# Layer 0's experts of a two-layer AdaLN kernel: all eight by every token, or the two chosen ones by gathered rows

## Time and profile before

| | us |
|---|---|
| median of 3 runs | 474.52 (472.8 to 476.28) |
| the profiled execution | 476.3 |
| its span, first to last instruction | 474.5 |
| PE, DVE, ACT, POOL busy | 426.4, 360.9, 336.2, 252.9 |
| mean granted TensorE clock | 0.845 |

### The profile page before, as it was taken

How to read it: one execution, slowest core, us unless ns; L and a number is a source line. 1 busy time by engine, 2 the same in 40 slices (tenths; PEclk the granted TensorE clock), 3 DMA queues, 4 the chain that set the end, 5 groups by cost and what they waited for, 6 DMA issues and landing times.

```text
span 474.5 us, 7765 instructions
## 1 busy us (share of the span) xinstructions
PE 426.4 (90%) x2212; PEld 285.5 (60%) x2212; DVE 360.9 (76%) x891; ACT 336.2 (71%) x898; POOL 252.9 (53%) x276
## 2 busy tenths in 40 slices
PE   8979778899899899886999889969989999999995
PEld 6667666676567677652433335324447887787883
DVE  4766795867898879689858896995848777879763
ACT  3364558787688686778998889968946566585552
POOL 3302238786866776822443543443418964766663
PEclk9997998999999999995565555555569999999999
DMA  6730021121134643633058344203114342433640
GB/s 185 207 112 2 0 79 57 44 92 56 35 114 108 164 149 103 123 87 114 12 90 118 96 98 131 60 5 102 24 22 149 127 126 81 141 128 92 183 130 22
DMA packets 45675, 44.68 MB, mean 94 GB/s; under 512 B 5557, under 2 KB 33789, under 8 KB 45633
## 3 DMA queue, kind: packets, MB, share of 16 engines
q1 hardware_dynamic: 45632, 44.19, 34.5%
HBM read 37.73 MB, written 6.44 MB: 93 GB/s over the span
## 4 chain that ended last, share of the span: by engine, by line
PE 43%; DVE 13%; issue 5%; ACT 3%; POOL 1%; POOLq 0%; DVEq 0%; ACTq 0%
PE P L1244 8%; PE P L1245 8%; PE P L1246 8%; PE P L1523 8%; PE P L1513 5%; DVE nm L902 4%; PE P L1380 1%; ACT EX L1179 1%; POOL hidl L469 1%; PE P L1349 1%; PE P L1268 1%; DVE O L917 1%; PE P L1374 1%; DVE kvs L697 1%; DVE SC L606 1%
## 5 line engine op out<-in xcount | busy, mean ns | idle before, releaser
L469 POOL TENSOR_TENSOR hidl<-tmp,hidh 128x512 fp32r<-128x512 f32 x116 | 149.3, 1296 | 76.6 <-ACT hidh L1131 73.9
L1179 ACT ACTIVATE EX<-P,nm 128x256 f32<-128x256 f32 x256 | 116.9, 496 | 12.5 <-DVE nm L902 12.2
L1131 ACT ACTIVATE hidh<-tmp 128x512 fp32r<-128x512 f32 x116 | 73.1, 630 | 44.8 <-DVE tmp L865 20.4
L902 DVE TENSOR_REDUCE nm<-P 128x4 f32<-128x1024 f32 x64 | 77.8, 1218 | 24.4 <-PE P L1513 24.0
L1523 PE MATMUL P<-EX,qs 128*32 128x256 f32 x512 | 66.8, 619 | 12.1 <-DVE O L917 12.0
L1244 PE MATMUL P<-XH,WH 128*128 128x512 f32 x176 | 76.1, 433 | 1.5 <-DVE tmp L974 0.6
L1245 PE MATMUL P<-XH,WL 128*128 128x512 f32 x176 | 70.1, 399 | 0.0
L1246 PE MATMUL P<-XL,WH 128*128 128x512 f32 x176 | 70.1, 398 | 0.0
L513 POOL TENSOR_TENSOR qs<-qT,rz 128x128 f32<-128x128 f32 x64 | 24.6, 406 | 81.5 <-DVE rz L910 81.5
L865 DVE TENSOR_TENSOR tmp<-P,G 128x512 f32<-128x512 f32 x64 | 43.6, 687 | 25.2 <-ACT P L1152 20.1
L1244 PE MATMUL P<-hidh,WH 128*128 128x512 f32 x124 | 50.7, 409 | 11.3 <-POOL hidl L469 9.8
(11 more groups left out here) (138 smaller groups left out, 670.7 us busy)
## 6 DMA issues: line engine op xcount, KB each, us to landing
G<-gate_rows SPq DMA_DIRECT2D x56, 256.0 KB, 3.3
kv_parts<-kvs SPq DMA_DIRECT2D x16, 256.0 KB, 2.4
VS<-kv_parts SPq DMA_DIRECT2D x48, 64.0 KB
KS<-kv_parts SPq DMA_DIRECT2D x48, 64.0 KB
G<-gate_rows SPq DMA_DIRECT2D x8, 224.0 KB, 3.0
G<-gate_rows SPq DMA_DIRECT2D x8, 192.0 KB, 3.3
G<-gate_rows SPq DMA_DIRECT2D x8, 160.0 KB, 2.6
X<-in_x SPq DMA_DIRECT2D x4, 256.0 KB, 2.9
```

What stands on the lines that cost most here:

```text
L469: nc.gpsimd.tensor_tensor(hidl[:, u % 3, :], source, hidh[:, u % 3, :].bitcast(fp32), ALU.subtract).then_inc(s["low_ready"], 1)
L902: v.tensor_reduce(nm1[:, g % 4, 2 * h:2 * h + 2, :], P[:, bank:bank + 2, :].rearrange("p j (h s) -> p (j h) s", h=2), AX.X, ALU.max, negat ...
L1131: sc.activation(hidh[:, u % 3, :], source, ACT.Copy).then_inc(s["high_ready"], 1)
L1179: last = sc.activation(ex1(g, j)[:, h * S:(h + 1) * S], P[:, bank_s1(g, j), h * S:(h + 1) * S], ACT.Exp, bias=nm1[:, g % 4, j, h:h + 1], a ...
```

## The change

Layer 0's experts are computed for the chosen rows alone, in plain fp32:

- The shared expert stays dense: `shared_ups` and `shared_down` per pair, added to X by `shared_experts` on VectorE.
- Tokens are handled in two *waves* of 1024. For a wave, TensorE counts with a triangular matrix how many tokens ahead of each have chosen the same expert (`ranks`), and VectorE makes of it a slot number for each token and choice (`destinations`): each expert's rows start at a multiple of 128, so that 23 tiles of 128 rows hold any split of 2048 rows.
- GpSimd scatters the rows of a wave to DRAM with 16 indirect DMAs (`scatter`), SyncE loads them tile by tile, TensorE computes each tile with its expert's weights, whose column is read from a register (`wave_columns`), and SyncE stores the result in its place. GpSimd gathers the two rows of each token with indirect DMAs (`gather`); `combine` weights and adds them (VectorE for pairs 0 and 1, GpSimd for 2 and 3).
- The weights `W1`, `W2` are no longer split. The hidden bias is added by VectorE from `B1`, a broadcast of all biases. The DRAM areas are filled with zeros first.
- The norm, q, k and v of the second attention: pair 0 within wave 1 (steps 14 to 19), pairs 1 to 3 within the attention.

The core of the diff:

```diff
+WAVES = 2
+QPW = NP // WAVES
+TPW = NT // WAVES
+WTOK = TOK // WAVES
+TILES = 2 * WTOK // D + E - 1
+XGR = 4
...
+COMBINE_AT = 14
+KV_AT = 18
...  (SyncE)
+            load(tri[:, :], a["tri"], "ld_b")
+            load(tab[:, :], a["tab"].partition_broadcast(128), "ld_b")
...
+            for w in range(WAVES):
+                sp.dma_start(scratch["xe"][w].rearrange("(i p) d -> p i d", p=128),
+                             WT[:, 0, 0:D].unsqueeze(1).broadcast_to([128, TILES, D])).then_inc(filled, 16)
             sp.wait_ge(s["rows_ready"], 1)
...
             sp.wait_ge(s["rows_out"], 16)
-            for l, dst in ((0, mrow0), (1, mrow1)):
+            load(B1[:, :], a["ub0row"].partition_broadcast(128), "ld_w1")
+            for l, dst in ((0, mrow0), (2, mrow5), (1, mrow1)):
...
+            for n in range(XGR, WAVES * TILES + 7):
+                if n < WAVES * TILES:
+                    tile_load(n)
+                if n >= 7:
+                    tile_store(n - 7)
+                if n - 4 == TILES + KV_AT + 1:
+                    kv_store(0, 0)
+                if n - 4 == TILES + KV_AT + 2:
+                    kv_store(0, 1)
+                    kv_load(0)
+            kv_store(1)
+            kv_load(1)
...  (GpSimd)
+            def scatter(w):
+                pool.wait_ge(s["dest_ready"], w + 1)
+                pool.wait_ge(s["rows_sb"], QPW * (w + 1))
+                pool.wait_ge(filled, 16 * WAVES)
+                for t in range(TPW):
+                    for k in range(2):
+                        nc.gpsimd.indirect_dma_start(scratch["xe"][w], bass.IndirectOffsetOnAxis(dest[:, w, t, k:k + 1], 0),
+                                                     SC[:, TPW * w + t, :], None).then_inc(scattered[w], 16)
...
+            scatter(0)
+            root(1, 3)
+            scatter(1)
+            stored_tiles(0)
+            for p in range(QPW):
+                for t in range(TPP):
+                    for k in range(2):
+                        gather(p, t, k)
+                if p == 0:
+                    root(2, 0)
...
             for g in range(NG):
-                if g == 3:
-                    root(2, NP - 1)
+                if g == 1:
+                    root(2, 1)
+                if g == 0:
+                    stored_tiles(1)
+                if g < 6:
+                    p, n = 2 + g // 3, g % 3
+                    for j in range(3 * n, min(3 * n + 3, 2 * TPP)):
+                        gather(p, j // 2, j % 2)
+                if g in (4, 7):
+                    combine(2 + g // 7)
...  (VectorE, the destinations)
+                link(v.tensor_tensor(over[:, :, :], count.unsqueeze(2).broadcast_to([128, E, E]),
+                                     tab[:, 0:E].unsqueeze(1).broadcast_to([128, E, E]), ALU.is_gt))
...
+                v.tensor_copy(dest[:, w, :, :], slot[:, :, :]).then_inc(s["dest_ready"], 1)
...  (VectorE, the tiles)
+            for n in range(WAVES * TILES):
+                w, i = tile(n)
+                if n >= 3:
+                    tile_out(n - 3)
+                if n == TILES:
+                    at = wave_columns(1)
+                bias(n, at[i])
...
+                    if i == 11:
+                        destinations(1)
...
+                if w == 1:
+                    if i == COMBINE_AT:
+                        combine(0)
+                        ln_stats(2, 0)
...  (ScalarE, the tiles)
+            for n in range(WAVES * TILES):
+                w, i = tile(n)
+                if n + 1 < WAVES * TILES:
+                    tile_in(n + 1)
+                if n >= 1:
+                    tile_back(n - 1)
+                tile_hidden(n)
...  (TensorE, the tiles)
+            tile_transpose(0)
+            for n in range(WAVES * TILES):
+                w, i = tile(n)
+                if n + 1 < WAVES * TILES:
+                    tile_transpose(n + 1)
+                if n == TILES:
+                    at[1] = wave_columns(1)
+                tile_up(n, at[w][i])
+                if n >= 1:
+                    tile_turn(n - 1)
+                if n >= 2:
+                    tile_down(n - 2, at[(n - 2) // TILES][(n - 2) % TILES])
+                if w == 0:
+                    if i == 1:
+                        route(0, 3)
+                    if i == 2:
+                        rows_back(2)
+                    if i == 4:
+                        weights_back(0, 2)
+                    if i == 6:
+                        shared_down(2)
+                    if i == 8:
+                        rows_back(3)
+                        weights_back(0, 3)
+                    if i == 10:
+                        ranks(1)
+                    if i == 12:
+                        shared_down(3)
```

More of the change, by code:

```diff
@@ L892, in _ @@
                         link(last)
-                    if i == 17:
-                        kv(TPP * (p - 1))
-                if p >= 2 and i in (0, 4, 6):
-                    kv(TPP * (p - 2) + (1, 2, 3)[i // 3])
+                    if i == KV_AT:
+                        kv(0, 1)
+                    if i == KV_AT + 1:
+                        kv(2, 3)
+            for n in range(WAVES * TILES - 3, WAVES * TILES):
+                tile_out(n)
             def maxima(g, h):
@@ new lines, in ranks @@
+            def ranks(w):
+                pe.wait_ge(s["m_ready"], QPW * (w + 1))
+                pe.wait_ge(s["ld_b"], 16 * N_LD["ld_b"])
+                claim(SIDE, "wcol_ready", w + 1)
+                n = TPW + 1
+                mm(P[:, SIDE, 0:n * E], tri[:, :], M[:, w, :, :].rearrange("p t e -> p (t e)"), start=True, stop=False)
+                for t in range(TPW):
+                    last = mm(P[:, SIDE, (t + 1) * E:n * E].rearrange("p (t e) -> p t e", e=E), ones[:, :],
+                              M[:, w, t, :].unsqueeze(1).broadcast_to([128, TPW - t, E]),
+                              start=False, stop=(t == TPW - 1))
+                last.then_inc(s["rank_ps"], 1)
@@ new lines, in tile_turn, with tile_down @@
+            def tile_turn(n):
+                pe.wait_ge(s["hg_ready"], n + 1)
+                claim(BANK_HT, "hgt_sb", n + 1)
+                for c in range(C0):
+                    last = nc.tensor.transpose(P[:, BANK_HT, c * D:(c + 1) * D], hg[:, n % 2, c * D:(c + 1) * D],
+                                               ident[:, :])
+                last.then_inc(s["hgt_ps"], 1)
+            def tile_down(n, at):
+                pe.wait_ge(s["hgt_sb"], n + 1)
+                claim(BANK_TY, "ty_sb", n + 1)
+                for c in range(C0):
+                    last = mm(P[:, BANK_TY, 0:D], hgt[:, n % 3, c * D:(c + 1) * D],
+                              W2[:, c * D:c * D + E * H0 + D][:, bass.ds(at, D)], start=(c == 0), stop=(c == C0 - 1))
+                last.then_inc(s["ty_ps"], 1)
@@ new lines, in _ @@
+            weights_back(0, 1)
+            pe.wait_ge(s["ld_up0"], 16 * N_LD["ld_up0"])
+            shared_ups(0)
+            ranks(0)
+            transpose_tokens(1, 2, MISC)
+            shared_ups(1)
+            pe.wait_ge(s["ld_down0"], 16 * N_LD["ld_down0"])
+            shared_down(0)
+            transpose_tokens(1, 3, MISC)
+            shared_ups(2)
+            route(0, 2)
+            shared_down(1)
+            shared_ups(3)
+            at = {w: None for w in range(WAVES)}
+            at[0] = wave_columns(0)
@@ L1506, in scores @@
+            n = WAVES * TILES
+            tile_turn(n - 1)
+            for m in (n - 2, n - 1):
+                tile_down(m, at[1][m - TILES])
             def scores(g, half):
```

779 lines of the change are left out of this document (453 added, 326 removed).

## The result

The kernel after takes **618.98 us** (617.14 to 621.57, 4 runs) against 474.93 of the kernel before beside it: ratio 1.3042, 95% interval 1.2974 to 1.3111. It is 144 us slower. The sign of the forecast was right, its size was not: 499 us said +25, and 619 lies far outside 466 to 540.

A forecast was written before the change was run, and what follows sets the result against it. The replaced stage was taken as dense TensorE work, so added waiting decides. First scores 11 us later plus attention 14 us longer made +25 on 476.3; less 1.8 for the median, 499 us, range 466 to 540.

The forecast's parts named there:

- wave 0 with its hole: From the first tile at 107.3 to wave 1's first tile at 158.7, including a 7 us stall between the waves.
- c: Time GpSimd needs per indirect DMA in scatters and gathers, taken as 1.2 us.
- the circle: Tile loop: gelu, two transposes, copy back, next gelu, with two hand-overs; 1.4 us a tile.
- Meanwhile TensorE has some 15 us of shared work, then nothing: Before the first tile: TensorE does 15 us of shared work while slots and scatter 0 are awaited.
- 23 T: A wave's 23 tiles at step T = 1.5 us, making 34.5 us.
- new stall of 7 us: Between the waves: scatter 1 ends at 153.8, wave 1's first tile is at 158.7, wave 0 ends at 151.8.
- 24 issues from 153.90 to 163.5, of which 8.4 are issuing, landing 2.4: Hand-over to attention: pair 0's key and value loads, after a 3.3 us store; TensorE idle some 9 us.
- 12 us more in TensorE's order: Attention: transposes, q and kv of two more pairs at half clock add 12 us.
- 5 us of late queries: Attention: gathers and combines on GpSimd stand in front of queries, making them 5 us late.
- at nothing, under TensorE's: Attention: VectorE's extra kv and norms, some 20 us, counted as free; without cover up to 8 us.
- Dear descriptors: Rival: c = 2.4 us per indirect DMA delays first scores by 38 and queries by 8 more; 546 us, chance 0.08.
- the clock: Rival: the tile loop runs at 1.2 GHz with a 2.4 us step; 548 us, chance 0.09.

The follow-up runs named there:

- e11: Kernel after with fourth pair's root first, pairs 1 to 3 handled earlier, plain DMAs for indirect ones and constant column offsets: 522.10 us (one run).
- e1: Kernel after with root(1, 3) and its statistics moved ahead of wave 0's scatters and destinations: 614.29 us.
- e2: Kernel after with the tiles' column offsets as program constants instead of values loaded into registers: 603.10 us.
- e3: Kernel after with the 64 indirect DMAs replaced by plain DMAs of the same size, without the permutation: 577.71 us.
- e7: Kernel after with GpSimd waiting for each indirect DMA of scatter(1) and of pairs 0 and 1's gathers to land before the next: 630.57 us (one run).
- e4: Kernel after with pair 0's combine and its q, k and v six tiles earlier in wave 1: 624.08 us (one run).
- e12: Kernel after with pair 1's keys and values early, in wave 1, and without the gathers and combines of pairs 2 and 3: 583.65 us.
- e5: Kernel after with pair 1 combined and projected in wave 1, pair 0 four tiles earlier, its loads sent between tile loads: 597.74 us.
- e10: Kernel after with fourth pair's root first, pairs 1 to 3 handled earlier, and plain DMAs for the 64 indirect ones: 541.20 us.
- e6: Kernel after with the splits of layer 1's weights two to four groups further back in GpSimd's list: 629.74 us (one run).

## Why the prediction was wrong, step by step

The forecast said +25, it is +144; some 120 us are missing. They lie here:

| step | forecast | measured | off by |
|---|---|---|---|
| first tile | 107.3 | 129.0 | +22 |
| wave 0 with its hole | 51.4 | 66.4 | +15 |
| wave 1 with its registers | 46.5 | 72.2 | +26 |
| hand-over | 8.8 | 17.7 | +9 |
| attention, to the first product of layer 1's experts | 159 | 207.6 | +49 |
| from there to the end | 124.5 | 124.4 | 0 |

**Right:** the direction, and the reason for it: little TensorE work saved in a dense stage, much waiting brought in. c = 1.26 us an indirect DMA against 1.2. The slots stood at 87.5 against 83.2, but by luck in part: `context0(0)` waited 1.56 us for mrow0 instead of 6, and VectorE then stood 3.8 and 4.6 us for TensorE's contexts, at a clock of 0.70 and 0.52, which the forecast had not. Layer 1's experts are unchanged. The step of a tile is 1.25 us at full clock, as TensorE's 1.19 us of work and not the 1.4 of the circle would have it, and 2.35 at half; 1.5 was a fair mean: e11, where little else disturbs the loop, needs 46.9 us for wave 0 against the forecast's 44.5 without the hole.

**The first tile.** The step that failed is "Meanwhile TensorE has some 15 us of shared work, then nothing". I had costed the scatters as a delay of the rows and had not looked at what stands behind them in GpSimd's list: `root(1, 3)`, and through it much of that shared work. e1 shows it: 15 of the 22 us. In the rest are the slots' 4.3 us and 4.7 us of registers, which I had charged to wave 1 alone (e2: 5.0).

**The waves.** The step that failed is the length of a wave as 23 T plus TensorE's other work: no term of it held that indirect DMAs could delay other engines' semaphores. The remote waits during scatter(1) and the two bursts of gathers are some 13, 8 and 5 us on the engine that waits longest; e3 and e7 take them away in two different ways. With plain DMAs the two waves take 111.3 us instead of 138.6 (e3), against the forecast's 97.9; with the registers' 3.6 us more than forecast, some 10 us stay unexplained. The forecast's "new stall of 7 us" between the waves is not there as such: scatter(1) ends at 181.3, but TensorE is at wave 0's own tiles until 195.4, since these were held.
**The hand-over.** "24 issues from 153.90 to 163.5, of which 8.4 are issuing, landing 2.4" took the landing of one transfer, a store of `kv_parts` at that the earlier trace rows, for that of 24 loads, of which no row gave one. They move 1.5 MB; from the first issue at 265.2 to the first scores it is 20.0 us, a rate of some 79 GB/s with the last tile stores in between; the 24 loads of pair 1 take 20.2 us too (324.9 to 345.1). The transfer sets it, and e4 shows that it also blocks the tiles if it is sent earlier. Whether its bytes or its many small packets (nearly all under 2 KB) bound it, no run tells.

**The attention** is the largest error. I counted what moves there as 12 us more in TensorE's order and 5 us of late queries. The 12 us were sized well (two whole pairs are 13.7 us of TensorE's work in e12); the waits were not in it. The prediction has the sentence "Before, kv of pairs 0 and 1 was stored and loaded under the experts", and prices only pair 0's hand-over: the kernel before entered this stage with two pairs of keys and values in place (kv_load of pair 1 was issued at 189.3, ahead of the first scores at 203.1), and the kernel after enters it with one. Its ninth group then waits for a chain that passes through every engine and a transfer of 1.5 MB, 24 us late; e5 takes that away and gains 21. The next eight groups take 36 us longer. e5, with 65 us for them, still has 31 of these; e12 puts 6.5 of the 31 down to combining, and its trace 21 to the projections, whose engines wait for each other in turn. That VectorE's extra work was to count "at nothing, under TensorE's" rested on a cover that wasn't there: TensorE itself stood waiting for VectorE. That the stage was nearly full on three engines before should have warned me: there was no room in it for work that is needed at once.

**The rivals.** "Dear descriptors" and "the clock" gave 546 and 548; neither is what happened, and both were lower than the truth. The clock played a part: 0.77 and 0.83 in the two waves, while it was 0.99 before. But wherever the loop is fed it runs at the upper level, with 0.33 of its 1.19 us being transposes: from 145 to 160 us, beside nothing, the clock is 1.00 and TensorE 13.96 of 15 us busy. The falls to half follow the waits (0.70 from 160 to 185, where updates are held).

```profile
145.00:160.00 15.00, 13.96 (x107) 12.11 (x106) 6.36 (x21) 7.28 (x24) 0.00 (x0) 1.00 0.20 57
160.00:185.00 25.00, 10.94 (x52) 8.64 (x53) 5.59 (x17) 3.29 (x11) 15.40 (x16) 0.70 0.19 59
```

What no run settles: the single shares don't add up strictly. e1 gives 15 us at the first tile and 5 at the end, e2 23 at the last tile and 12 to 16 at the end, and the indirect form (e3, e10) costs 41 in one order and 53 in another. A stage entered earlier waited a little more in it each time.

## What to carry to other kernels

Cost an operation on an in-order engine by what is queued behind it, not by its own length: here 20 us of scatters held one pow on 128 x 4 elements, and with it VectorE and TensorE. When work is moved across a stage boundary, ask how far ahead the next stage used to be supplied; losing a lead of one pair cost some 21 us (e5), more than all the register loads (e2: 16). And a long idle time ahead of an instruction is no proof that moving it helps: e6 moved what GpSimd waited for, GpSimd stood as long for something else, and a load held back elsewhere cost 11 us.

## What the runs showed of the hardware

- An indirect DMA of 128 rows of 512 bytes holds GpSimd 0.96 us and comes every 1.26; a plain one of the same bytes every 0.53.
- Back to back, and with other engines at work, indirect DMAs went with semaphore updates of TensorE that came up to 11 us late (done at 170.38, seen at 181.34), while the DMA engines were busy 19% (160 to 185 us). Plain DMAs at twice the rate, to consecutive rows, had none, nor did indirect ones 2.5 us apart or more. The kernel after shows none in scatter(0), where VectorE and TensorE stood; e1, which has them work there, shows it.
- Loading 23 registers with bounds stops TensorE for 8.6 us, 0.37 each (at wave 1, and at wave 0 in e1; at wave 0 of the kernel after 4.7 show); using them costs next to nothing (a step of 1.25 us against 1.22).
- Twenty-four transfers of 64 KB (1.5 MB) in one queue took some 20 us from the first issue until the last was in use, twice, and a tile load queued behind them was waited for 18.3 us (e4).
